# Key tile's heads padded to 376 elements: a half's read in 750-byte pieces instead of runs of 6000 bytes

## What is computed

```python
q = _split_heads(query @ Wq.T + bq)
k = _split_heads(key @ Wk.T + bk)
v = _split_heads(value @ Wv.T + bv)
scores = jnp.einsum('bhqd,bhkd->bhqk', q, k)
scores = scores * tau[:, :, None, None] + delta[:, None, None, :]
scores = scores / jnp.sqrt(jnp.asarray(DK, scores.dtype))
p_attn = jax.nn.softmax(scores, axis=-1)
x = jnp.einsum('bhqk,bhkd->bhqd', p_attn, v)
```

## Time and profile before

| | |
|---|---|
| median of 3 runs | 443.85 us (442.79 to 444.97) |
| profiled execution | 443.59 us |
| its span | 441.7 us, 8239 instructions |
| busy TensorE, VectorE, ScalarE, GpSimd | 77%, 57%, 46%, 45% of the span |
| mean granted TensorE clock | 0.84 of full |
| DMA packets, bytes | 36695, 52.24 MB |
| share of the 16 DMA engines: q1, q10 | 31.5%, 9.0% |

### The profile page before, as it was taken

The page is one execution under the profiler, slowest core; times in us unless marked ns, Lnnn a source line. Parts: engine busy times, 40 slices in busy tenths (PEclk is TensorE's granted clock), DMA queues, the critical chain, the costliest instruction groups (busy, mean ns, idle before and its releaser), DMA issues.

```text
span 441.7 us, 8239 instructions
## 1 busy us (share of the span) xinstructions
PE 339.7 (77%) x2713; PEld 262.7 (59%) x2713; DVE 251.7 (57%) x561; ACT 202.9 (46%) x543; POOL 197.1 (45%) x244
## 2 busy tenths in 40 slices
PE   6638498694996996995986868955451699999993
PEld 2415375573865865864856647542331598989982
DVE  3264346779589698787897884474417432322320
ACT  2402565595693783874964738233120233242320
POOL 3631503695375564745844917246131213232422
PEclk9566789899798897998998989565555599999999
DMA  8781654616417427637367112897720302111121
GB/s 255 286 206 29 141 133 85 153 37 156 115 31 144 100 41 150 180 88 174 83 123 194 28 32 88 301 381 241 245 79 3 95 0 66 28 59 49 31 62 37
DMA packets 36695, 52.24 MB, mean 118 GB/s; under 512 B 10495, under 2 KB 28744, under 8 KB 36390
## 3 DMA queue, kind: packets, MB, share of 16 engines
q1 hardware_dynamic: 27948, 34.69, 31.5%
q10 hardware_dynamic: 7056, 12.41, 9.0%
q0 software_dynamic: 1648, 4.59, 3.5%
HBM read 42.81 MB, written 9.31 MB: 118 GB/s over the span
## 4 chain that ended last, share of the span: by engine, by line
PE 54%; DMA 13%; DVE 11%; POOL 8%; issue 7%; ACT 3%; ACTq 2%; SPq 2%; DVEq 0%; POOLq 0%
PE ps L580 50%; DMA W<-nmT 7%; PE ps L584 4%; DMA d_q<-hold 2%; DVE hold L1611 2%; ACTq L1179 2%; POOL W L1479 2%; POOL W L1470 2%; POOL W L1487 2%; DMA W<-d_delta 1%; DMA prepi<-in__lenS 1%; SPq L507 1%; ACT hold L1000 1%; DVE mx L1714 1%; DMA out_x<-hold 1%
## 5 line engine op out<-in xcount | busy, mean ns | idle before, releaser
L580 PE MATMUL ps<-W 125*32 125x112 f32 (+2 forms) x1280 | 90.9, 267 | 43.0 <-DMA W<-nmT 30.8
L580 PEld LDWEIGHTS ps<-W 125*32 125x32 f32 (+2 forms) x1280 | 68.1, 127 | 65.7 <-DMA W<-nmT 34.1
L1714 DVE TENSOR_REDUCE mx<-ps 112x2 f32<-112x750 f32 x64 | 59.9, 936 | 38.9 <-PE ps L580 38.1
L1188 ACT ACTIVATE W<-ps 125x448 f32<-125x448 f32 x96 | 50.8, 542 | 39.2 <-PE ps L580 38.8
L580 PE MATMUL ps<-hold,proj 128*128 128x128 f32 (+2 forms) x288 | 55.9, 343 | 3.1 <-ACT W L1107 2.0
L1362 ACT ACTIVATE hold<-ps,consts 128x128 f32<-128x128 f32 x88 | 25.0, 370 | 50.2 <-PE ps L580 50.2
L580 PEld LDWEIGHTS ps<-hold,proj 128*128 128x128 f32 x288 | 40.1, 201 | 12.5 <-issue 3.8
L584 PE MATMUL ps<-consts,hold 112*128 112x112 f32 (+3 forms) x136 | 28.8, 303 | 22.8 <-DMA hold<-d_x,hold 5.6
L1591 POOL DMA_INDIRECT out_x<-hold x11 | 16.3, 1479 | 62.5 <-DVE hold L1992 60.0
L580 PE MATMUL ps<-hold 128*128 128x128 f32 (+4 forms) x256 | 37.4, 299 | 8.5 <-DVE hold L1611 5.8
L580 PE MATMUL ps<-proj,hold 128*125 128x256 f32 (+1 forms) x128 | 41.7, 468 | 1.1 <-ACT hold L1082 1.0
(11 more groups left out here) (167 smaller groups left out, 574.0 us busy)
## 6 DMA issues: line engine op xcount, KB each, us to landing
W<-in_L_ffn_W SPq DMA_DIRECT2D x10, 1024.0 KB, 11.4
W<-in_L_ffn_W ACTq DMA_DIRECT2D x6, 1024.0 KB, 6.8
d_k<-W SPq DMA_DIRECT2D x16, 281.2 KB, 3.5
W<-d_k SPq DMA_DIRECT2D x16, 281.2 KB
hold<-in_ctxT SPq DMA_DIRECT2D x8, 375.0 KB, 3.8
W<-d_k SPq DMA_DIRECT2D x16, 187.5 KB
W<-d_q SPq DMA_DIRECT2D x48, 56.0 KB, 3.2
d_x<-hold ACTq DMA_DIRECT2D x8, 224.0 KB, 2.6
```

The lines of the kernel that those rows point to most:

```text
L580: return pe.matmul(o, lhsT=l, rhs=r, start=start, stop=stop, skip_group_check=True)
L1188: act.activation(pexp[g % 2][0:LT, t, :], pE[n % 2][0:LT, 0:HG * T], ACT.Exp).then_inc(exp_done, 1)
L1714: dve.tensor_reduce(mx[:, 2 * i:2 * i + 2], pS[0:T, :, 0:L], X, ALU.max).then_inc(mx_done, 1)
```

## The change

A head's slot in kst gets LP = 376 elements instead of 375. p_kread keeps the same four DMAs for a half, but source and destination are given with the head as a dimension of its own, and the destination is cut to the first 375 elements of a slot. The matmul that reads all positions of a head is cut in the same way. The two loads of ones into the key stacks grow from 3000 to 3008 words a row, and so does the array that is read. The slices of a_scoresT need no change in the text; they begin at the new head pitch of 752 bytes.

```diff
+    LP = L + 1
...
-        kst32 = [carve(NH * L // 2) for _ in range(2)]
+        kst32 = [carve(NH * LP // 2) for _ in range(2)]
...
-                src = d_k[b % 2][m].rearrange("t (d h) l -> (t d) (h l)", h=HM)
-                dst = kst[b % 2][:, HM * m:HM * m + HM, :]
+                src = d_k[b % 2][m].rearrange("t (d h) l -> (t d) h l", h=HM)
+                dst = kst[b % 2][:, HM * m:HM * m + HM, 0:L]
                 for lo, n in ((0, 3), (48, 2), (80, 1)):
-                    sp.dma_start(dst[lo:lo + 16 * n].rearrange("p h l -> p (h l)"), src[0:16 * n]).then_inc(kst_loaded[2 * m + b % 2], 16)
+                    sp.dma_start(dst[lo:lo + 16 * n], src[0:16 * n]).then_inc(kst_loaded[2 * m + b % 2], 16)
...
-                sp.dma_start(kst32[i][KD:KX], A["ones"][:, 0:NH * L // 2]).then_inc(ones_loaded, 16)
+                sp.dma_start(kst32[i][KD:KX], A["ones"]).then_inc(ones_loaded, 16)
...
-                    last = mm(pS[0:T, n, 0:L], qst[b % 2][0:KD, 2 * i + n, :], kst[b % 2][0:KD, 2 * i + n, :], True, True)
+                    last = mm(pS[0:T, n, 0:L], qst[b % 2][0:KD, 2 * i + n, :], kst[b % 2][0:KD, 2 * i + n, 0:L], True, True)
...
-    laid["ones"] = _np.full((3, 3000), 0x3F803F80, _np.uint32).view(_np.float32)
+    laid["ones"] = _np.full((3, 3008), 0x3F803F80, _np.uint32).view(_np.float32)
```

## The result

The changed kernel takes 446.98 us (median of 4 runs, 444.27 to 450.88), the kernel before 443.32 us beside it: a ratio of 1.0139, with a 95% interval of 1.0078 to 1.0200. It is slower by more than the 0.5% that a measurement can tell from no change. The forecast was 445.0 us and "same" as the likeliest, with a range of 438 to 450 us; the time lies in the range, and the direction went to the rival "each piece is paid in full". The profiled execution took 448.53 us with a span of 446.7 us; the execution is 4.9 us longer than the profiled one of before.

A forecast was written before the change was run, and what follows sets the result against it. Half the span was TensorE's matmuls, 7% the exposed nmT transfer, where the change acts. Nine places at 0.12 us gave +1.1 us on 443.59, so 444.7; with the median 0.26 above, 445.0 us, range 438 to 450.

The forecast's parts named there:

- each piece is paid in full: Rival: the first-half key read beside nmT costs the engines' 0.39 us, nine times 3.5 us, say 448 us; chance 0.31.
- The place: The change acts where SyncE's key and query reads lie beside nmT of batches 1 to 6, some 3 us each.
- I take 0.12 us, a third of the engines' price: Added time of one key half's read cut into 768 pieces, assumed mostly covered because something other than the engines holds the stage.
- the full price: 0.39 us more for a key half, if the engines' own time for 750-byte pieces sets the pace.
- the bound under load: Twice 0.39 us for a key half, if a piece's surcharge grows under load as the bytes do.
- nine places: Batch 0's query read, nmT of batches 1 to 6, batch 1's second half, one late second half: 9 x 0.12 us.
- The deciding point of the rival: Each piece is paid once the first half's stage drops from 218 GB/s to below some 190.
- SyncE: Issuing the key reads: each part stays one instruction, nothing added; the key write with 384 pieces takes 0.38 us to issue.
- The rule on unaligned starts: DRAM reads not starting at multiples of 256 bytes fetch extra: 0.37 us a half, sum 3.3 us; set aside.
- The turns that let nmT through: Rival: engines alternate between queues, so nmT waits behind shorter pieces: 6.8 us saved over batches 1 to 6, 437 us; chance 0.22.
- TensorE and clock: Score matmul pairs stay at 0.49 us; a batch moving to the longer 1.2 GHz stretch costs up to 1.7 us, outside the sum.
- The second halves: Twelve other key halves, hidden by unknown cover; without it 12 x 0.39 = 4.7 us, so the range goes further up.

The follow-up runs named there:

- e5: Changed kernel with only the first key half read in 750-byte pieces, the second in runs of 6000 bytes: ratio 1.0119 to the kernel before.
- e6: Changed kernel with only the second key half read in 750-byte pieces, the first in runs of 6000 bytes: ratio 0.9996 to the kernel before.
- e9: Kernel before, with SyncE waiting for the previous batch's nmT to land before it reads the first key half: ratio 1.0735 to the kernel before.
- e4: The changed kernel run once more, 768 pieces of 750 bytes a half: ratio 1.0152 to the kernel before.
- e8: Key tile of the kernel before, the gap moved to DRAM rows of 376 elements, read in 750-byte pieces: ratio 1.0191 to the kernel before.
- e3: Changed kernel with padding behind every 2 heads, 384 pieces of 1500 bytes a half: ratio 0.9989 to the kernel before.
- e12: Changed kernel with each head cut into thirds with gaps, 2304 pieces of 250 bytes a half: ratio 1.1081 to the kernel before.
- e2: Changed kernel with padding behind every 4 heads, 192 pieces of 3000 bytes a half: ratio 0.9971 to the kernel before.
- e7: Changed kernel with d_k rows of 768 bytes in DRAM, so pieces start at multiples of 256 bytes: ratio 1.0002 to the kernel before.
- e11: Changed kernel with d_k rows of 768 bytes and the whole array shifted by 128 bytes: ratio 1.0065 to the kernel before.

## Why the prediction was right or wrong

The time lies in the range, but "same" in the sense of the forecast, within 0.5%, did not come, and the sum of +1.1 us was about a third of the measured +3.7 (446.98 against 443.32).

**The place: right.** The first half's read beside nmT is where the change is paid. e5 against e6 shows that the same pieces cost 1.2% there and nothing in the second half, and e9 that nmT takes 1.8 us when no key read is beside it.

**"I take 0.12 us, a third of the engines' price": the step that failed.** An nmT piece grew by 0.52 us on average (3.12 us over six) and the first query read by 0.64 us. In e4, e5 and e8 the nmT pieces grew by 0.27, 0.42 and 0.64 us. That is two to five times my 0.12, around the 0.39 us that I called the full price, and inside the bound under load (twice 0.39). Two choices led there. I took the surcharge of a piece from the key write; under load it is 24 to 26 ns instead of 8. And I argued that an engine waiting for something else has room for the piece. It had room for 384 pieces a half, as e3 shows, not for 768. Why a piece costs more the more of them are under way was not tried; that the price is 16 ns in e3, 24 in e4 and 40 for the shorter packets of e12 is measured, its mechanism is open.

**Two more terms.** I counted nine places; the second half of batch 1 is not in the changed kernel's chain. And I left the clock out of the sum: the stretches between the nmT pieces, where it shows, grew by 1.4 us in one profile of the changed kernel and by 3.8 in the other.

**The deciding point of the rival was a bad one.** I said that below some 190 GB/s in the first half's stage each piece is paid. One early microsecond of the stage in the changed kernel, 137.0 to 138.0, shows 205 GB/s, and one that starts 0.1 us earlier 178. Such a window cannot decide. Over the whole stage the rates are 179 before and 151 after, so a point of 190 GB/s lay above both. The cost per byte that I had read from one microsecond, 71 ps, was sound: the whole stage gives 73.

**SyncE: wrong in the number, right in the effect.** A part is issued in 610 ns instead of 416, so a half's issue is 0.6 us longer. I had taken the key write's 0.38 us as the model for a pattern with three dimensions. e2 and e3 show that it costs nothing measurable by itself.

**The rule on unaligned starts.** The Trainium skill's page "DMA: Bandwidth & Descriptors", section "How a descriptor splits into AXI transactions", would have given 0.37 us a half, nearer to what was lost than my 0.12. The aligned starts of e7 left the engines' time within 2.4 us of the changed kernel's (153.0 against 155.4 in e4), and moving every start by 128 bytes did not change it (153.1 in e11). So the runs do not agree with the rule as the cause, though its size was of the right order. I had set the key write against it, and that was no test: the rule is about what is fetched, and the key write's side in DRAM is written.

**The turns that let nmT through: did not come.** nmT's pieces grew. The earlier trace rows had been the right row for this: transfers issued earlier on the other queue hold back a later one, whatever their pieces. **TensorE and clock:** the score matmuls of a pair still take 0.48 us, as called. The mean granted clock of the two profiled executions is 0.840 and 0.838, but a mean over the span hides the slow stretches, which lie elsewhere in the two; in e4 the mean is 0.827, and 3.1 us of the loss lie in a stretch at 0.77.

**The second halves** were rightly called the way further up: in the changed kernel one became late, by 0.9 us in one profile and hardly at all in the other; in e12 there are seven such waits.

## What to carry to other kernels

When a transfer is cut finer, price it in the stage in which it runs, over the whole time from issue to landing of what waits behind it, and not from a window inside or from a transfer that runs alone: here a piece cost 8 ns in the key write and 24 to 26 under load. Ask which small, awaited transfer lies behind the large one; the same added packets cost 1.2% beside it and nothing elsewhere. Compare start times along the chain and not sums of waits, which can add up to the right total by accident, and look at the clock stretch by stretch, not by its mean. And look at both transfers that share a layout: a total of zero, as in e7, need not mean that the read costs nothing.

## What was not expected of the hardware

- The same bytes written to DRAM rows 768 bytes apart instead of 750 landed in 2.7 us (e7) instead of 3.3 to 3.5 (384 pieces of 750 bytes), and in 2.9 us with every start 128 bytes off (e11).
- A DMA's issue on SyncE's queue takes 416 ns with one run per row and 590 to 610 ns with an inner dimension of 2 to 8 pieces on both sides, nearly the same for 3000, 1500 and 750 bytes (medians of 48).
- Added pieces occupy the engines for 16 ns each at 384 pieces a half, 24 to 26 at 768 and 40 at 2304 pieces of 250 bytes.
- The same kernel in two executions showed the 1.2 GHz clock in different stretches: in batch 6 the mean granted clock was 0.93 in one and 0.77 in the other, 25.2 us against 28.2 for the same matmuls.
